# Two items each of experts 0 and 1 run beside the last batch's way to the router, in an attention and mixture-of-experts block

## The reference

```python
mod = (silu(c) @ wmod).reshape(4, 6, 1, -1)          # sa, ca, ga, sb, cb, gb
ga = (2 * (ga >= 0) - 1) * maximum(abs(ga), 0.25)    # gb likewise
h = layernorm(x) * (1 + ca) + sa
x = x + ga * attention(h)      # rms-normed q, k; softmax; y minus its part along v; Wo
h = layernorm(x) * (1 + cb) + sb
probs = softmax(h @ router_w.T)                      # [2048, 8]
w = top_p(probs, 0.9)          # the likeliest experts until their sum passes 0.9
for e in range(8):
    out += (silu(h @ gate_w[e].T) * (h @ up_w[e].T)) @ down_w[e].T * w[:, e:e+1]
x = x + gb * out
```

## Time and profile before

| | us |
|---|---|
| median of 3 runs | 574.07 |
| lowest, highest | 573.63, 577.67 |
| the profiled execution's own time | 577.54 |
| its span, first to last instruction | 575.7 |
| mean granted clock of PE | 0.897 |

### The profile page before, as it was taken

One profiled execution on the slowest core, in us unless ns is written; L12 is line 12 of the kernel. 1 busy time (PEld: TensorE's weight loads), 2 busy tenths in 40 slices (PEclk: granted clock), 3 DMA queues, 4 the chain that ended last, 5 costly groups with the idle time before them and its releaser, 6 DMA issues.

```text
span 575.7 us, 10183 instructions
## 1 busy us (share of the span) xinstructions
PE 471.9 (82%) x3338; PEld 352.7 (61%) x3339; DVE 353.3 (61%) x823; ACT 260.7 (45%) x351; POOL 188.6 (33%) x228
## 2 busy tenths in 40 slices
PE   3847989897999799895305689999997999999980
PEld 3333333343444343334305689989997999999980
DVE  2595486579559946758487274747575466575440
ACT  2214778556876688671000253535342535363320
POOL 1026030012001202000001246666666467676642
PEclk9956999799999899796555699999999899999996
DMA  8440000000200022120230245656665374845432
GB/s 269 143 147 1 0 2 2 0 1 1 74 1 2 1 74 85 62 74 0 73 86 29 76 139 123 166 114 162 126 158 132 61 183 93 200 83 101 73 59 33
DMA packets 33349, 46.18 MB, mean 80 GB/s; under 512 B 5668, under 2 KB 24868, under 8 KB 33320
## 3 DMA queue, kind: packets, MB, share of 16 engines
q0 software_dynamic: 11936, 22.50, 19.2%
q1 hardware_dynamic: 21384, 23.30, 12.8%
HBM read 32.86 MB, written 12.93 MB: 80 GB/s over the span
## 4 chain that ended last, share of the span: by engine, by line
PE 61%; DVE 16%; issue 12%; DMA 5%; ACT 2%; POOL 2%; DVEq 0%; POOLq 0%; SPq 0%; ACTq 0%
PE psS L1356 23%; PE psY L1369 10%; PE psY L1286 6%; PE psS L1177 4%; PE psM L1127 4%; PE psM L1152 3%; DMA h_sel<-h_rows,idx_in 3%; PE psM L1342 2%; PE psM L1222 2%; DMA out<-y_sel,idx_out 1%; PE psM L1244 1%; DVE xhat L681 1%; ACT probs L531 1%; DVE one_row L993 1%; PE psM L1115 1%
## 5 line engine op out<-in xcount | busy, mean ns | idle before, releaser
L531 ACT ACTIVATE probs<-psS 128x1024 f32<-128x1024 f32 x128 | 123.4, 1027 | 29.7 <-PE psS L1177 29.0
L1356 PE MATMUL psS<-hs_hi,w_hi 128*128 128x256 f32 x400 | 115.0, 287 | 6.9 <-issue 3.6
L1356 PE MATMUL psS<-hs_lo,w_hi 128*128 128x256 f32 x400 | 114.0, 285 | 0.0
L1356 PE MATMUL psS<-hs_hi,w_lo 128*128 128x256 f32 x400 | 113.8, 285 | 0.0
L424 POOL DMA_INDIRECT out<-y_sel,idx_out x50 | 87.6, 1753 | 45.5 <-DVE y_sel L1059 35.4
L1356 PEld LDWEIGHTS psS<-hs_hi,w_hi 128*128 128x128 f32 x400 | 77.1, 193 | 8.6 <-issue 8.5
L1356 PEld LDWEIGHTS psS<-hs_hi,w_lo 128*128 128x128 f32 x400 | 77.2, 193 | 0.0
L1356 PEld LDWEIGHTS psS<-hs_lo,w_hi 128*128 128x128 f32 x400 | 77.1, 193 | 0.0
L1286 PE MATMUL psY<-probs,v_aug 128*32 128x512 f32 x512 | 72.3, 638 | 0.1
L411 POOL DMA_INDIRECT h_sel<-h_rows,idx_in x50 | 51.2, 1025 | 43.4 <-PE psM L1342 23.1
L1177 PE MATMUL psS<-qT,kT 64*128 64x512 f32 x256 | 54.4, 487 | 7.5 <-ACT probs L531 6.4
(11 more groups left out here) (176 smaller groups left out, 755.8 us busy)
## 6 DMA issues: line engine op xcount, KB each, us to landing
w_in<-gateT SPq DMA_DIRECT2D x8, 512.0 KB, 4.0
w_in<-upT SPq DMA_DIRECT2D x8, 512.0 KB, 4.7
w_in<-downT SPq DMA_DIRECT2D x8, 512.0 KB, 4.2
x_all<-x SPq DMA_DIRECT2D x4, 512.0 KB, 5.7
mod_rows<-mod_table SPq DMA_DIRECT2D x4, 512.0 KB, 6.8
h_rows<-h_nat SPq DMA_DIRECT2D x4, 512.0 KB, 3.5
out<-x_all SPq DMA_DIRECT2D x4, 512.0 KB, 4.5
h_rows<-mod_rows POOLq DMA_DIRECT2D x4, 512.0 KB
```

The source lines that it names most:

```text
L531: act.activation(probs[:, gk % 4, 2 * pair:2 * pair + 2, :], psS[:, pair, :, :], ACT.Exp, scale=ATT_SCALE).then_inc(probs_done, 1)
L1356: mm = pe.matmul(ps[:, i * SW:(i + 1) * SW], w, v[:, k, :], start=at == 0, stop=at == 3 * KC - 1)
```

## The change

1. Four items are taken ahead: two of expert 0 and two of expert 1, each from the kept tokens of the first three batches only (`EARLY = 4`, `TILES0 = 12`). In the last batch's steps 12 to 15 PE ranks these tokens and makes two short lists. After the last step, the tail of the last batch, the ranking of all tokens, the eight late lists and items 0 to 3 form one hand-written order on each engine (`last_batch_and_first_items`). The late lists leave out what the early ones hold, and the loop starts at item 4.
2. Routing is rebuilt: the comparison of experts works on logits in bf16 flags, the kept mask is formed without dividing, running totals are accumulated by PE (1 + 12 and 1 + 16 matmuls) instead of by hops on DVE, ACT copies the lists to `idx_all`.
3. Modulation: the gates are bounded once, on 4 partitions, before batch 0's loop (`modulate_rows`). The attention gate is multiplied into the output weights (`w_og`, on GpSimd), so `add_attention` adds straight from PSUM. Eight more matmuls make columns of the second scale and shift; PE turns the normalised rows and ACT applies the columns (`take_h`). The rows for `h_rows` are scaled and shifted by GpSimd. The gate rows go from DRAM to DRAM.
4. Weights of expert 1 are loaded and split beside items 0 and 1; those of expert 2 are rounded after expert 1's one late item. `downs` puts both token tiles in one PSUM bank and signals near its end.

```diff
@@ DVE, batches 1 and 2
             def add_attention(p):
-                    dve.tensor_tensor(h_nat[:, tt, :], psM[:, tt // 2, (tt % 2) * C:(tt % 2 + 1) * C], ga,
-                                      ALU.mult).then_inc(o_gated, 1)
...
+                    dve.tensor_tensor(two, tail_ps(p, i), two, ALU.add).then_inc(x2_done, 1)
@@ GpSimd
+            def gate_outputs(p):
+
+                if p:
+                    pool.wait_ge(o_ps, 2 * p)
+                pool.tensor_tensor(w_og[:, :, :], w_o[:, :, :], mod_rows[:, GATE_ROW + p:GATE_ROW + p + 1, :].broadcast_to([P, KC, C]),
+                                   ALU.mult).then_inc(w_gated, 1)
+
+            def experts_input(p):
+                wide = lambda at: mod_rows[:, at + p:at + p + 1, :].broadcast_to([P, TT, C])
+                pool.wait_ge(xhat2_done, (p + 1) * TT)
+                if p:
+                    pool.wait_ge(h_out, 16 * p)
+                pool.tensor_tensor(h_nat[:, :, :], xhat[:, :, :], wide(SCALE_ROW), ALU.mult).then_inc(h_scaled, 1)
+                pool.wait_ge(h_scaled, p + 1 + 2)
+                pool.tensor_tensor(h_nat[:, :, :], h_nat[:, :, :], wide(SHIFT_ROW), ALU.add).then_inc(h_done, 1)
...
+            pool.wait_ge(h_out, 16 * LAST)
+            pool.wait_ge(w_out, 16)
+            pool.wait_ge(scattered, GATES)
+            pool.wait_ge(consts, NCONST)
+            pool.wait_ge(listed0, 1)
             for k in range(S):
+                pool.indirect_dma_start(h_sel[:, k, :], None, h_rows[0:LAST * N, :],
+                                        bass.IndirectOffsetOnAxis(ap=idx_all[:, k:k + 1], axis=0)).then_inc(gathered, 16)
+            read_list(1)
+            gather(1)
+            read_list(2)
+            gather(2)
+            root(LAST)
+            experts_input(LAST)
+            read_list(3)
+            gather(3)
+            pool.wait_ge(x2_out, 16 * LAST)
+            write_list(0)
+            scatter(0)
+            write_list(1)
+            scatter(1)
+            pool.wait_ge(idx_ready, 1)
+            pool.wait_ge(h_last_out, 16)
+            pool.wait_ge(w_out, 32)
+            read_list(4)
+            gather(4)
@@ PE, the last batch's steps
+                    if gk == 1:
+                        turn_y(p, G - 1, False, True)
+                    elif gk == 3:
+                        turn_outputs(p, False)
+                    elif gk == 5:
+                        project_outputs(p, False)
+                    elif gk == 6:
+                        turn_last_y(0)
+                    elif gk == 8:
+                        turn_h(p, 0, False)
+                        pe.wait_ge(yn_done, LAST * G + 1 + G)
+                        turn_h(p, 1, False)
+                    elif gk == 10:
+                        route(p)
+                    elif gk == 11:
+                        turn_last_y(1)
+                    elif gk == 12:
+                        pe.wait_ge(yn_done, LAST * G + 2 + G)
+                        rank_tokens(psM[:, 1, :], 0)
+                    elif gk == 13:
+                        turn_last_y(2)
+                    elif gk == 14:
+                        list_early(0)
+                        list_early(1)
@@ PE, after it
+            def last_batch_and_first_items():
+                turn_last_y(G - 1)
+                pe.wait_ge(yn_done, LAST * G + 3 + G)
+                turn(0)
...
+                gate_up(0, 0, 0)
+                gate_up(0, 0, 1)
+                turn(1)
+                pe.wait_ge(y_sb, B * G + 2)
+                turn_outputs(LAST, False)
+                pe.wait_ge(sel_lo, 2)
+                gate_up(1, 0, 0)
+                project_outputs(LAST, False)
+                gate_up(1, 0, 1)
+                turn(2)
+                downs(0, 0)
+                pe.wait_ge(w_ready, 6)
+                pe.wait_ge(sel_lo, 3)
+                gate_up(2, 1, 0)
+                turn_h(LAST, 0, False)
+                turn_h(LAST, 1, False)
+                gate_up(2, 1, 1)
+                route(LAST)
+                turn(3)
+                downs(1, 0)
+                pe.wait_ge(sel_lo, 4)
+                gate_up(3, 1, 0)
+                rank_tokens(psY[:, 1, :], 1)
+                gate_up(3, 1, 1)
+                list_tokens(0)
+                downs(2, 1)
+                for e in range(1, 4):
+                    list_tokens(e)
+                turn(4)
+                for e in range(4, E):
+                    list_tokens(e)
@@ DVE, after the last batch
+                product(3, 0)
+                places()
+                tiles_of_places()
+                rows_of_places(0)
+                product(3, 1)
+                count_items()
+                rows_of_places(1)
+                output(2, 2)
+                rows_of_places(2)
+                rows_of_places(3)
+                split_input(4)
+                take_weights(4)
+                split_hidden(3, 0)
+                split_hidden(3, 1)
+                for e in range(4, E):
+                    rows_of_places(e)
@@ ACT and DVE, between experts
                 if half == 0:
-                    act.wait_ge(down_ps, 2 * before + FREE)
-                    round_weights(e + 1, 1)
+                    with act.If(e2 > 0):
+                        act.wait_ge(down_ps, 2 * before + FREE)
+                        round_weights(e + 1, 1)
```

More of the change, by code:

```diff
@@ L126, in adaln_block @@
[L126 to L138, removed]
@@ L188, in adaln_block @@
         y_sel = sb("y_sel", [P, S, C])
+        for parts, part in ((w_hi, "w_hi"), (w_lo, "w_lo")):
+            parts.append([sb(f"{part}1_{n}", [P, I * KC], F32R) for n in range(3)])
         psS = ctx.enter_context(nc.psum_tensor("psS", [P, 2, 2, 512], F32))
@@ L932, in _ @@
[L932 to L946 removed]
+            at = [0]
@@ L1064, in body, with body_of_item @@
+            def body_of_item(e, e2, first, m, half):
                 product(m, 0)
@@ L1068, in body @@
                 split_hidden(m, 0)
-                if first and half == 0:
-                    with dve.If(e2 > 0):
-                        output(e, m - 1)
-                else:
-                    output(e if first else e + 1, m - 1)
+                output(e if first else e + 1, m - 1)
                 split_hidden(m, 1)
@@ new lines, in rank_tokens @@
+            def rank_tokens(ps, n):
+                pe.wait_ge(consts, NCONST)
+                pe.wait_ge(rt_kept, n + 2)
+                pe.matmul(ps[:, 0:(NT + 1) * E], earlier[:, :], keep_b[:, :, :].rearrange("p t e -> p (t e)"), start=True, stop=False)
+                tiles = (TILES0, NT)[n]
+                for t in range(tiles):
+                    mm = pe.matmul(ps[:, (t + 1) * E:(NT + 1) * E].rearrange("p (t e) -> p t e", e=E), ones_b[:, :],
+                                   keep_b[:, t:t + 1, :].broadcast_to([P, NT - t, E]), start=False, stop=t == tiles - 1)
+                mm.then_inc(rank_ps, 1)
@@ L1383, in body @@
                 turn(m + 1)
-                if first and half == 0:
-                    with pe.If(e2 > 0):
-                        downs(m - 1, 1)
-                else:
-                    downs(m - 1, 1 - half if first else half)
+                downs(m - 1, 1 - half if first else half)
+            attention(pe, body)
+            last_batch_and_first_items()
             pe.wait_ge(meta_ready, 1)
-            turn(0)
-            walk_items(pe, body, lambda *a: None)
-            items = pe.value_load(meta[0:1, 2, E - 1:E], min_val=E, max_val=ITEMS)
+            walk_items(pe, body_of_item, lambda *a: None)
+            items = pe.value_load(meta[0:1, 2, E - 1:E], min_val=EARLY + E, max_val=EARLY + ITEMS)
             downs(items - 1, 1)
```

950 lines of the change are left out of this document (571 added, 379 removed).

## The result

The changed kernel takes 579.13 us (median of 17 runs, 576.49 to 580.63), the kernel before 574.58 (17 runs, 572.36 to 578.29): ratio on record 1.0066, 95% interval 1.0045 to 1.0088 (the two medians alone give 1.0079). So it is slower by some 0.7%, where the forecast was 554 us, in 543 to 567. The profiled execution has a span of 577.9 us against 575.7. The kernel before was profiled in an execution 3 us above its median, so the traces show 2.2 us between the kernels where the medians show 4.6 and the ratio 3.8.

A forecast was written before the change was run, and what follows sets the result against it. PE was taken to bound the items and a chain of latencies the 66 us before them; 3.0 - 4.5 - 2.6 + 4.0 - 26.3 + 6.4 = -20.0 us from the 574.07 median gave 554 us, range 543 to 567.

The forecast's parts named there:

- batches 1 and 2: Attention: less VectorE work gains 1.3 us a batch, -2.6; GpSimd's scalings, 5 us a batch, covered by the next batch.
- batch 0's end: Gates no longer stand before batch 1's normalisation, so PE's turn of x need not wait: -4.5 us (2.8 to 4.8).
- Rival B: GpSimd and VectorE in each other's way, VectorE standing for one of two scalings a batch: 567 us; chance 0.17.
- Item 4 to item 6: Late items of experts 0 and 1: 5.4 us for expert 2's weight rounding plus 1 us of skips, +6.4.
- The skips: Two jumps over unused expert bodies on every engine, between items 4 and 6: 1 us (0 to 5).
- The start: Before the second batch's first value matmul: extra modulation matmuls, VectorE operations and gates, +3.0 us.
- the last batch: Last attention batch: xhat, mask, ranking matmuls and early lists lengthen its chain, +4 us (-1 to +9).
- the hole: Last value matmul to item 4: early items' PE work fills the latency chain, 103.6 us to 77.3, 26.3 less.
- signs of being wrong in size: Mixed stretch's clock under 0.8, PE waiting over 15 us at the lists, or attention stages exceeding 60, 55 and 47 us.
- A: Rival, fewer waits: the stretch to item 4 takes 67 us and the skips are free, 543 us; chance 0.22.
- C: Rival, the clock: waits in the mixed stretch hold PE at a low clock, 581 us; chance 0.04.
- D: Rival, no earlier start: early items lie in a row behind the last router as before, 574 us; chance 0.05.

The follow-up runs named there:

- gp_later: The changed kernel, but GpSimd starts its scalings in batches 1 and 2 only once VectorE has finished the second group's correction; 567.53 us, ratio 0.9863.
- gp_pieces: The changed kernel with each GpSimd scaling cut from one operation of 1024 columns into four of 256, in all four batches; 568.86 us, ratio 0.9887.
- straight: gp_later with the one-item passes of experts 0 and 1 written out ahead of the loop over expert pairs; 563.95 us, ratio 0.9825.
- straight_early: straight with expert 2's gate and up weights rounded behind item 4 instead of item 5; 556.55 us, ratio 0.9701.
- gather_first: gp_later with GpSimd reading item 3's list, starting its gather and listing item 0's outputs before scaling the last batch's rows; 568.01 us, ratio 0.99.
- scale_on_dve: The changed kernel with VectorE again scaling and shifting the rows of batches 0 and 1; 571.78 us, ratio 0.9934.
- early_rows: straight_early plus VectorE making the rows of places of experts 4 and 5 before splitting item 4's input; 554.74 us, ratio 0.9652.
- best: early_rows plus gather_first's edit, and VectorE writing the modulation rows behind batch 1's normalisation; 553.37 us, ratio 0.9631 against the kernel before.

## Why the prediction was wrong

**The step that failed** is the one on batches 1 and 2: "The price is on GpSimd ... The cover is the 50 us to the next batch". The price of 2.5 us an operation was right (2.36 and 2.42), and who waits for h_nat was right. What the cover leaves out, and the sum put at nothing, is who can't run while GpSimd does. A VectorE instruction with two SBUF inputs stood for 1.6 to 2.7 us beside each scaling, in the correction of the values, which is on PE's path. With batch 0's end it said -7.1 for both batches; the changed kernel had +6.0, gp_later -7.1. Once GpSimd was out of the way, moving that work off VectorE was worth what the prediction said. Batch 0's end was right as well: PE's turn of x has no wait there any more.

**Rival B** had the mechanism, with 0.17, and too small a price: VectorE "for one of two scalings" in each batch, 5.0 us for batches 1 and 2. VectorE stood for both and for w_o's gate, 4.3 us a batch, and of the 13.1 us between the two traces 7.6 were clock, of which B had nothing. In the last batch it cost nothing: beside the two scalings there, 246.34 to 251.17 us, VectorE runs one copy from PSUM. In the stretch to item 4 there is one case of it, a_lo with 4.92 us. The Trainium skill, "SBUF — State Buffer", Who interferes with whom, says that a VectorE instruction with two SBUF inputs and a GpSimd one that reads SBUF exclude each other for the whole instruction. The trace and gp_pieces agree: 2.06 us beside one long operation, 0.43 beside short ones. By the Trainium skill, "GPSIMD Engine Reference", 3.1, I had estimated 2.25 us a scaling; the rows have 2.36 and 2.42. A row that could have moved the chances was there: 6.00 us where 1.37 do. I read it as a stall of the start. It is another pair, though, VectorE's normalisation with one large input beside iotas, which have none; it shows that an instruction of VectorE can be held up beside GpSimd, not that the correction would be.

**Item 4 to item 6** came to +12.8, not +6.4. The wait for w_lo was right (5.9 against 5.4). The skips were sized at 1 us with 0 to 5; they took 4.2 before item 5 alone, near the 5.0 of the row that I had named and not taken. straight, without the jumps, took 5.5 us less in the stretch. The remaining 1 to 2 us I put down to the half clock behind each stop (0.21 us a matmul from 364.41 us on). straight_early shows that w_lo's wait was an order of work.

**The start** (+2.5 for 3.0), **the last batch** (+3.8 for 4.0) and **the hole** (-24.0 for -26.3) held. Of the hole's terms the wait for the gather of item 3 was 3.3 for 1.2, and the rows of places 8.3; the clock there, 0.80, is at the bound that I had set. One sum in it is 0.3 us too long (9.8 + 5.7 + 21 x 0.09 is 17.4, not 17.7), which decides nothing. Of the signs of being wrong in size one appeared: batch 2, with 61.2 us, exceeded its 55. Item 4 came at 348.3 instead of 334 (333.6 by the terms), 12.4 of it from attention and 2.3 its own. **From item 6 on** took 1.1 more, 0.6%, which no experiment looked into; kernels that change nothing there had 195.3 (gather_first) to 197.5 us (scale_on_dve), so it may be no more than the difference between executions.

**The sum** is 13.1 and 6.4 us of misses, 2.3 of the hole and 1.1 at the end, less 0.7 of start and last batch: 22.2 us, the distance between +2.2 and -20.0. Nothing points to A (the stretch to item 4 took 79.6 us, not 67), to C (in the windows of 5 us from 285 to 310 us, with items 0 to 2, the clock was 1.00; it was 0.50 from 275 to 280 and from 340 us on) or to D (item 0 began 10.1 us behind the last value matmul). That early_rows and best land at 555 and 553 doesn't make the forecast right: they have a wait and an order that the change lacks.

## What to carry to other kernels

Before work is moved from VectorE to GpSimd, list what VectorE runs in the next few microseconds. If that has two SBUF inputs and is on the path, the move can cost the length of the GpSimd instruction; place it behind a semaphore where VectorE reads PSUM, or cut it into short instructions. When a loop's bodies are skipped because the work was done elsewhere, count the jump as a wait (here some 4 us), and look again at which weights were loaded or rounded under the items that are gone.

## What the runs showed of the hardware

- A GpSimd operation with two SBUF inputs, 128x1024 in f32, takes 2.35 to 2.43 us in batches 1 and 2, and up to 2.99 on the way to item 4 (gather_first); four of 256 columns take 2.85 to 3.11.
- VectorE's instruction of two SBUF inputs beside it goes from 0.42 to 2.06 or 2.52 us, a pair from 0.49 to 3.15; copies and casts from PSUM stay at 0.68 and 0.69. In gather_first an operation of 32 columns went from 0.19 to 2.69.
- VectorE's normalisation, one large SBUF input, four times 256 columns, took 1.38 us alone, 1.80 beside GpSimd's copies and 2.75 beside these and the gate of w_o (scale_on_dve).
- Before item 5, where the engines jump over the unused bodies of an expert with one item, PE stood for 3.8 to 4.2 us and the profile names no releaser; the same pass written straight, without reading the counts, had no such gap.
- Behind a stop of PE of 2.6 us in batch 2 the granted clock was 0.50 in the changed kernel and in gp_later. In gp_later it was 1.00 again from 196 us, 3.3 us after PE had begun to work; in the changed kernel, with a further stop of 1.80 us in between, only 13 us after. Why it wasn't back before that further stop isn't shown.
